# A sparse feed-forward on one Trainium2 core: at most two row scatters under way at a time

## What is computed

```python
x = x + jnp.tanh(g_xattn[0]) * _L0_xattn_ref(_layernorm(x), ctx_2048, ...)
x = x + jnp.tanh(g_ffn[0]) * _L0_ffn_ref(_layernorm(x), ...)
x = x + jnp.tanh(g_xattn[1]) * _L1_xattn_ref(_layernorm(x), ctx_2048, ctx_2048, ...)
x = x + jnp.tanh(g_ffn[1]) * _L1_ffn_ref(_layernorm(x), ...)
```

```python
topk_w, topk_idx = jax.lax.top_k(softmax(x @ gate_w.T), 4)     # then made to sum to 1
combine = (one_hot(topk_idx, 16) * topk_w[..., None]).sum(1)
shared = (silu(x @ g.T) * (x @ u.T)) @ shared_down.T * sigmoid(x @ shared_gate_vec.T)
sparse = sum over the 16 experts e of (silu_mul(x @ w_gu[e].T) @ w_d[e].T) * combine[:, e]
return shared + sparse
```

## Time and profile before

| | us |
|---|---|
| median of 3 runs (1669.72 to 1674.21) | 1672.87 |
| the profiled execution, its own time | 1672.83 |
| its span, first to last instruction | 1671.1 |
| PE busy in it | 1492.4 (89%) |
| DVE busy | 1275.9 (76%) |
| ACT busy | 1041.1 (62%) |
| POOL busy | 830.2 (50%) |

### The profile page before, as it was taken

How to read it: one execution, slowest core, us unless ns; L and a number is a source line. 1 busy time by engine, 2 the same in 40 slices (tenths; PEclk the granted TensorE clock), 3 DMA queues, 4 the chain that set the end, 5 groups by cost and what they waited for, 6 DMA issues and landing times. The chain is left out here.

```text
span 1671.1 us, 39908 instructions
## 1 busy us (share of the span) xinstructions
PE 1492.4 (89%) x11666; PEld 1158.1 (69%) x11666; DVE 1275.9 (76%) x4644; ACT 1041.1 (62%) x3249; POOL 830.2 (50%) x1256
## 2 busy tenths in 40 slices
PE   0589999999999999999948869999599999999998
PEld 0478889888898888889834436777456666555554
DVE  5589999999999999999858545666378887565564
ACT  5578887788888887888733435555266777233322
POOL 0666666666666666766512773444466564000000
PEclk9999999999999999999969989999799999799999
DMA  7494300000000000000011643443322110000000
GB/s 304 154 232 105 76 0 0 0 0 0 0 0 0 0 0 0 0 0 1 2 68 49 208 149 117 126 127 120 137 62 69 61 61 9 1 12 2 14 13 14
DMA packets 75235, 95.69 MB, mean 57 GB/s; under 512 B 32139, under 2 KB 60299, under 8 KB 73607
## 3 DMA queue, kind: packets, MB, share of 16 engines
q1 hardware_dynamic: 68278, 75.53, 15.6%
q0 software_dynamic: 6864, 19.01, 3.1%
HBM read 62.74 MB, written 40.43 MB: 62 GB/s over the span
## 5 line engine op out<-in xcount | busy, mean ns | idle before, releaser
L665 ACT ACTIVATE prob<-bS,ntop 128x128 f32<-128x128 f32 x512 | 186.7, 420 | 4.1 <-DVE ntop L474 4.0
L569 POOL TENSOR_TENSOR rs<-ve,half 128x6 f32<-128x6 f32 x128 | 178.0, 1390 | 0.0
L649 ACT COPY pT<-bP 128x512 f32<-128x512 f32 x128 | 75.7, 591 | 144.1 <-PE bP L331 144.1
L577 POOL TENSOR_SCALAR kv<-kv,rs,nb 128x128 f32<-128x128 f32 x256 | 151.5, 598 | 27.5 <-POOL nb L572 27.5
L451 DVE SCALAR_TENSOR_TENSOR qn<-qn,mv,rs 128x128 f32<-128x128 f32 x512 | 155.5, 364 | 6.4 <-POOL rs L569 4.8
L322 PE MATMUL bS<-kT,qT 128*128 128x128 f32 x1024 | 138.2, 278 | 10.7 <-ACT prob L665 10.7
L298 PE MATMUL bq<-w,xq 128*128 128x256 f16 x1024 | 133.9, 274 | 6.5 <-DVE xq L423 6.5
L636 ACT ACTIVATE qT<-bqT,vecs 128x256 f32<-128x256 f32 x256 | 134.8, 595 | 3.4 <-PE bqT L282 3.3
L322 PEld LDWEIGHTS bS<-kT,qT 128*128 128x128 f32 x1024 | 126.1, 194 | 13.9 <-issue 12.6
L1819 ACT ACTIVATE l_prob<-l_sc,l_ntop 128x128 f32<-128x128 f32 x256 | 99.6, 391 | 55.0 <-DVE l_ntop L1874 53.7
L665 ACT ACTIVATION_READ_ACCUMULATOR prob<-bS,ntop 128x1 f32 x512 | 133.4, 261 | 0.0
(11 more groups left out here) (313 smaller groups left out, 4315.4 us busy)
## 6 DMA issues: line engine op xcount, KB each, us to landing
f_xblk<-by_slot SPq DMA_DIRECT2D x79, 132.0 KB, 2.1
by_slot<-zeros SPq DMA_DIRECT2D x1, 10112.0 KB, 35.6
l_back<-by_pick SPq DMA_DIRECT2D x16, 512.0 KB, 3.5
f_wstage<-by_expert SPq DMA_DIRECT2D x16, 480.0 KB, 3.5
l_piece<-in_f_w SPq DMA_DIRECT2D x16, 312.0 KB, 2.8
wo_stage<-in_wproj SPq DMA_DIRECT2D x8, 512.0 KB, 4.3
by_expert<-in_f_w SPq DMA_DIRECT2D x18, 128.0 KB, 2.8
x<-in_x SPq DMA_DIRECT2D x1, 2048.0 KB, 7.7
```

Of the source, the lines that this page charges most:

```text
L569: nc.gpsimd.tensor_tensor(rs[:, t, :], ve[:], r["half"][:, 0:6], ALU.pow).then_inc(rs_ready, 1)
L577: done = nc.gpsimd.tensor_scalar(key, key, rs[:, t, 4 + j:5 + j], nb[:, t, j:j + 1], ALU.mult, ALU.add)
L665: done = nc.scalar.activation(prob[:, t, h, :], bS[:, h, :], ACT.Exp, bias=ntop[:, t, h:h + 1], accum_out=total[:, t, h:h + 1])
```

## The change

One semaphore for the scatters becomes two, used in turn. Before scatter n, POOL waits until the semaphore of its parity shows that scatter n-2 has landed (16 for each scatter landed on it). SP's wait before the routed half becomes two waits, each for 32 scatters. Nothing else changes: not the transfers, nor their order, nor the buffers.

```diff
-                 "shifted_r", "ex_r", "step", "mask_r", "ranked", "rows_r", "owner_r", "scattered",
+                 "shifted_r", "ex_r", "step", "mask_r", "ranked", "rows_r", "owner_r",
+        scattered = [m.sem(f"{tag}_scattered{i}") for i in range(2)]
...
-            sp.wait_ge(s["scattered"], 16 * B * K)
+            for done in scattered:
+                sp.wait_ge(done, 16 * B * K // 2)
...
             for b in range(B):
                 for k in range(K):
+                    n = b * K + k
+                    reach(pool, scattered[n % 2], 16 * (n // 2))
                     nc.gpsimd.indirect_dma_start(by_slot, bass.IndirectOffsetOnAxis(ap=rows[:, b, k:k + 1], axis=0),
-                                                 xn[:, b, :], None).then_inc(s["scattered"], 16)
+                                                 xn[:, b, :], None).then_inc(scattered[n % 2], 16)
```

## The result

The changed kernel takes 1694.46 us (median of 4 runs, 1694.2 to 1696.07) against 1673.21 for the kernel before on the same chip: a ratio of 1.0132, 95% interval 1.0116 to 1.0148, or +21 us. The prediction was 1697.0, range 1683 to 1708. The profiled execution spans 1692.8 us, 21.7 more than before.

The account below looks back on a forecast made before the run. The prediction took the 64 scatters, ending some 10 us behind the shared half, to bound this place. Quiet pairs +6.2, loads +21 and give-back -3 made +24.2 us on 1672.83: 1697.0 us, range 1683 to 1708.

Parts of the forecast that it names:

- What bounds this place: Around the first feed-forward: the 64 scatters end the first part, some 10 us behind the shared half; nothing hides them.
- Nothing taken away, no cost of the wait as such: Same 64 scatters in the same order; SP's wait in two parts and one more semaphore cost nothing.
- The quiet term, +6.2: Scatters where no other transfer runs: a pair takes 2.73 us for 2.53, 31 x 0.20 = +6.2 us, bounds 0 and 6.2.
- The loads' term, +21: Scatters beside the experts' loads: each load holds them about 2.2 us, costing 1.5; 14 loads give +21 us, bounds 5.6 to 31.
- The chance phase of 0.7 us: At a load, the next scatter's data is due on average 0.7 us after the load's begins, leaving 1.5 of 2.2 us.
- Equal turns: Rival: loads and scatters share DMA engines evenly, 0.4 us a load; 1675 to 1682 us, about 1679; chance 0.12.
- a way out for equal turns: Trace's 74.3% to 9.2% of the DMA engines contradicts equal turns unless the two queues' packets differ much in size.
- What comes back, -3: POOL's 12.7 us of long writings beside DVE's splits shrink under the limit: -3 us, bounds 0 and -12.7.
- The other half of the term: Some lateness of POOL's long writings falls into time in which POOL would wait for a landing; part of the -3 us.
- The sum: Whole kernel: 6.2 + 21 - 3 = +24.2 us on 1672.83, giving 1697.0 us.
- The clock was no term: PE's granted clock is already down at 0.50 in the idle time; a longer idle stretch adds nothing.
- The signs named beforehand: New trace: some 60 POOL waits, quiet starts 2.5 to 2.75 us apart, 14 load waits of 1.5 to 2, writings 74.1 or less.

Follow-up runs that it names:

- the halves: Kernel before with earlier row numbers on DVE, and each of DVE's 16 splits made in two halves: 1696.23 us, ratio 1.0148.

## Why the prediction was right, and where its terms were off

**What bounds this place.** Right. The scatters end the first part, the shared half ends at 991 to 993 us with the change and without it, and in eleven of the twelve experiments SP's first block load follows the landing of the last scatter. In the twelfth, the halves, the shared half took over. (With eight under way the profiled execution took 1682.76 us, 10 more than the others would give, nearly all of it behind the first feed-forward.)

**Nothing taken away, no cost of the wait as such.** Right: the kernel with eight under way equals the kernel before.

**The quiet term, +6.2.** The mechanism and its price were right: a landing takes 1.47 us behind a writing, a restart 0.27 (0.28 taken from the earlier trace rows), so 2.70 a pair for 2.53. The term should have been 31 x 0.17 = 5.3. The kernels without loads and splits show it at 9.2 - 4.1, about 5. In the changed kernel itself only half of the scatters stand where no load runs: from 981.6 us on, 30 gaps come to 11.9 us where 30 of 0.30 are 9.1, so 2.8 are extra (POOL's group, 981.6 to 1023 us):

```profile
L1282 POOL DMA_INDIRECT by_slot<-f_xn,f_rows x30 | 29.4, 978 | 11.9 <-DMA by_slot<-f_xn,f_rows 11.6 <-issue 0.3
```

**The loads' term, +21.** The mechanism was right, the size was too large. Of the 21.1 us of waits beyond 19.2, 18.3 stand in front of 981.6 us, where the loads are: 1.3 us a load, with whatever the instruction packets cost there. I had 1.5, and the quiet term on top. The 14 long waits there are 0.98 to 2.34 us. A second pair of kernels gives the loads alone: without splits, the limit's idle time is 44.3 with loads and 28.4 without, and 15.9 / 14 = 1.14 us a load. The chance phase of 0.7 us spares part of the 2.2 (0.54 MB at 0.47 MB in 2.0 us is 2.3, rather); what spares the rest was not separated. With three under way it is 0.57 a load, since more of a hold is covered, and with one under way 0.98, or about 0.9 without the 1.2 us at 985.50. Equal turns of the queues, 0.4 us a load, are refuted by all three.

The prediction left a way out for equal turns: packets of very different size. Its own rows answer that. SP's 176 packets with 0.47 MB and POOL's 18 with 0.08 MB are on average about 2.7 and 4.4 KB (an estimate from those figures), which is no ratio of one to eight. DMA views of the kernel before, 948.4 to 950.2 us and 951.3 to 952.6, show SP's queue alone, though a scatter had left POOL at 948.27 and another at 950.81; beside the second no split runs, so it is not DVE that holds the data:

```profile
q1 hardware_dynamic: 106, 0.41, 89.7%
```

```profile
q1 hardware_dynamic: 66, 0.25, 80.8%
```

The hold is not as complete at each load: in the changed kernel, 929 to 930.8 us, the shares are 57.9% and 35.6%. What decides it stays open.

**What comes back, -3.** The busy time of the writings, the sign named beforehand, went the wrong way: +1.2. The step that failed is the one from "fewer writings meet such an instruction" to time given back. Fewer did (by the start times in the two traces 13 of 64 begin inside a split, 17 before), but each lost more, 0.96 us where it was 0.58, since a writing that is released by a landing begins anywhere in the split, while one of a busy POOL mostly begins late in it (median 0.87 us into the split before, 0.22 now). The other half of the term, lateness that falls into waits, seems right: the limit adds 25.1 us of waits without splits and 21.1 with them, though the loads come faster in the kernels without. Taken together, from the first scatter to the first block's load, the limit costs 24.2 us without splits and 22.3 with them, so some 2 us did come back. Without loads it is the other way: the splits raise the limit's cost from 8.6 to 15.1. This term depends on the phase between POOL and DVE, and its sign can't be read from shares of busy time.

**The sum.** 21.1 of waits and 1.2 of writings are 22.3 for a forecast of 24.2 (27.2 of waits, 3 given back); the scatters' start, 0.9 us early by chance, leaves 21.4. Two errors partly cancelled: 6 us too much for waits, 4 too little for writings. That the total came within 3 us is in part luck. The clock was no term, as forecast: 0.50 until PE works again, and 1.00 some 6 us later.

**The signs named beforehand.** The starts in the quiet stretch are 2.68 to 2.70 us apart over two places in the last 24 scatters (forecast 2.5 to 2.75). POOL waits for scatters 45 times, not some 60: where a long writing or a wait has just let the other scatter land, there is none. There are 14 long waits for 14 loads, but half of them are 0.98 to 1.25 us and not 1.5 to 2. The busy time of the scatters' line is 75.3, not 74.1 or less. The shared half ends at 991.1, a us earlier than named. The routed half kept its length.

## What to carry to other kernels

A limit on transfers under way costs the part of a landing that is not covered by the issuer's own pace, and it is decided by the slowest landing, not the median one: here two places of 1.26 us are 2.53 against 2.70 of writing, landing and restart, short by 0.17 a pair, and far short of a landing that stands behind another queue's load. Count the places from the worst landing in the stretch: three left 6 us, eight nothing. Before limiting, ask who would gain; here nobody did, for ACT's wait for the loads is 45.1 us with the limit and 45.4 without.

## What was not expected of the hardware

- Fetching instructions seems to delay transfers. One of the 16 DMA engines was busy for about 0.96 us with one packet of the instruction queue, and POOL waited 0.9 to 2.1 us longer for a scatter under way at that time. The kernel before has three such packets too, and POOL, which waits for no landing there, loses nothing; with two under way three such places cost 4.1 us.
- POOL's writing of a scatter's orders waits for the end of a DVE instruction with two inputs in the on-chip memory if it begins inside it (2.23 us for 0.96), and not at all if it began before. This cost 10 us of the 94.8 in the kernel before. DVE's splits were not seen to wait for a writing.
- A wait that is already met is free on POOL: 63 gaps of 0.30 us with 56 such waits (eight under way) as with none.
